# Two reciprocals later on VectorE, one residual sum earlier on GpSimd, and the third norm's squares ahead of four signs on ScalarE

## The reference

```python
qkv = layernorm(x) @ W_qkv.T              # q, k, v per head; k is normalised again per head
# per head, at each of 512 positions t:
F_t = retention * F_{t-1} + coef * v_t k_t^T     # 16 x 16, elementwise factors
y_t = (W_LTM + F_t) q_t
x1  = x + layernorm(y @ W_o.T)
h   = square(relu(layernorm(x1) @ W_fc.T))       # 1024 wide
u   = h @ W_proj.T
# 5 steps of a leaky neuron driven by u; s = spikes / 5
out = x1 + layernorm(s)
```

## Time and profile before

| | us |
|---|---|
| median of 3 runs | 570.86 (570.71 to 573.21) |
| the profiled execution's own time | 573.23 |
| its span, first to last instruction | 571.4 |
| VectorE busy | 514.7 (90% of the span) |
| TensorE busy, matmuls | 478.8 (84%) |
| GpSimd busy | 385.7 (67%) |
| ScalarE busy | 366.4 (64%) |
| mean granted clock of TensorE | 0.914 of full speed |

### The profile page before, as it was taken

How to read it: one execution, slowest core, us unless ns; L and a number is a source line. 1 busy time by engine, 2 the same in 40 slices (tenths; PEclk the granted TensorE clock), 3 DMA queues, 4 the chain that set the end, 5 groups by cost and what they waited for, 6 DMA issues and landing times.

```text
span 571.4 us, 7792 instructions
## 1 busy us (share of the span) xinstructions
PE 478.8 (84%) x2245; PEld 318.6 (56%) x2252; DVE 514.7 (90%) x746; ACT 366.4 (64%) x901; POOL 385.7 (67%) x206
## 2 busy tenths in 40 slices
PE   4683587759999798979898999989997989897992
PEld 2451244426576566736574657656674657465881
DVE  5799999999997999899897999899989998797767
ACT  4561323664677977887768887896879736863331
POOL 1138978687848977696868795888679694783022
PEclk9686557858989999999899999999999989999997
DMA  7475577457484559547774749454934588410002
GB/s 263 130 205 145 147 208 197 147 148 186 135 215 96 149 124 278 146 130 184 216 196 124 177 114 276 143 145 118 285 109 125 153 244 217 111 39 7 30 2 73
DMA packets 54778, 87.64 MB, mean 153 GB/s; under 512 B 5456, under 2 KB 19408, under 8 KB 54736
## 3 DMA queue, kind: packets, MB, share of 16 engines
q1 hardware_dynamic: 54160, 87.12, 56.3%
q10 hardware_dynamic: 576, 0.03, 0.1%
HBM read 78.74 MB, written 8.39 MB: 152 GB/s over the span
## 4 chain that ended last, share of the span: by engine, by line
PE 59%; DVE 15%; issue 9%; ACT 9%; POOL 5%; DMA 1%; SPq 0%; DVEq 0%; ACTq 0%; POOLq 0%
PE p_c L382 15%; PE p_c L412 12%; DVE state L982 8%; PE p_a L312 7%; PE p_y L360 7%; PE p_c L373 6%; POOL prod L1250 4%; PE p_a L333 3%; ACT sign L713 2%; PE p_y L351 2%; PE p_u L552 1%; ACT oo L615 1%; DVE p_u L972 1%; PE p_a L342 1%; DVE yf L1202 1%
## 5 line engine op out<-in xcount | busy, mean ns | idle before, releaser
L1250 POOL TENSOR_TENSOR prod<-state,qf 128x1024 f32<-128x1024 f32 x127 | 300.3, 2380 | 117.6 <-PE p_y L360 69.3
L982 DVE TENSOR_TENSOR_SCAN state<-ret,p_u 128x512 f32<-128x512 f32 x256 | 308.7, 1209 | 0.0
L972 DVE TENSOR_TENSOR p_u<-vrep,p_k 128x512 f32<-128x512 f32 x256 | 171.5, 676 | 0.1
L382 PE MATMUL p_c<-wproj_sb,ht 128*128 128x256 f32 x448 | 100.4, 379 | 0.0
L382 PEld LDWEIGHTS p_c<-wproj_sb,ht 128*128 128x128 f32 x448 | 84.0, 190 | 12.0 <-ACT yf L626 0.8
L312 PE MATMUL p_a<-xt,wqkv_s 128*128 128x512 f32 x276 | 84.8, 448 | 3.0 <-POOL xt L1266 1.6
L412 PE MATMUL p_c<-x1t,wfc_s 128*128 128x512 f32 x324 | 81.6, 398 | 1.8 <-ACT hr L697 1.1
L360 PE MATMUL p_y<-prod,summer 128*32 128x512 f32 x512 | 73.9, 652 | 9.1 <-POOL prod L1250 8.0
L312 PEld LDWEIGHTS p_a<-xt,wqkv_s 128*128 128x128 f32 x276 | 54.9, 208 | 42.1 <-issue 15.5
L412 PEld LDWEIGHTS p_c<-x1t,wfc_s 128*128 128x128 f32 x324 | 59.3, 188 | 22.8 <-issue 7.3
L713 ACT ACTIVATE sign<-yf,drive_sb 128x512 bf16<-128x512 f32 x60 | 38.1, 709 | 0.2
(11 more groups left out here) (190 smaller groups left out, 614.7 us busy)
## 6 DMA issues: line engine op xcount, KB each, us to landing
vrep<-v_rows SPq DMA_DIRECT2D x256, 256.0 KB, 4.7
xa<-in_x SPq DMA_DIRECT2D x9, 512.0 KB, 4.8
v_rows<-vf SPq DMA_DIRECT2D x16, 256.0 KB, 2.5
x<-in_x SPq DMA_DIRECT2D x7, 512.0 KB, 6.8
out<-x SPq DMA_DIRECT2D x7, 512.0 KB, 3.3
ht<-in_w_fc SPq DMA_DIRECT2D x1, 1024.0 KB, 7.6
wproj_sb<-in_w_proj SPq DMA_DIRECT2D x1, 1024.0 KB, 10.3
state<-in_w_qkv SPq DMA_DIRECT2D x1, 512.0 KB, 6.0
```

Source lines behind the costliest of these rows:

```text
L382: last = pe.matmul(p_c[(u + 1) % 2][:, 0:D], ht[:, f, tokens(u)], wproj_sb[:, f, :], start=(f == 0), stop=(f == FT - 1))
L972: v.tensor_tensor(p_u[n % NU][:, :], vrep[:, n % NV, :], p_k[:, :], ALU.mult).then_inc(S["hebb_done"], 1)
L982: v.tensor_tensor_scan(state[:, s % NS, i, :], ret[:, r:r + 1].broadcast_to([P, L]), p_u[n % NU][:, :], 0.0, ALU.mult, ALU.add).then_inc(S ...
L1250: p.tensor_tensor(prod[:, s % NZ, :, :], state[:, s % NS, :, :], qf[:, s // HS, :].unsqueeze(1).broadcast_to([P, 2, L]), ALU.mult).then_in ...
```

## The change

The third norm's reciprocal, `scales(3, b1)`, stays in slot 8 of VectorE's order but moves behind both `hebbian` and the first `scan` of that slot. The first norm's, `scales(1, b)`, moves from slot 3 to slot 4, behind `key_reciprocal(g, 1)`. On GpSimd `add_attention(b1)` moves from slot 6 to slot 5, which is in front of `read(g, 5)` instead of behind it. On ScalarE `squares_x1(b1)` and `deviation(3, b1)` move in front of `copy_yf(b2, 2)` and `copy_key(g)`, and of the five signs of the first pair only one stays before them; the other four come behind `copy_xt(b, 0)`. The second load of x for the last element gets a semaphore of its own, `last_in`, in place of `again_in`. No instruction is added or taken away but for semaphore waits.

```diff
--- before.py
+++ after.py
@@ -162,7 +162,7 @@
         p_c = [ps(f"p_c{i}", [P, L]) for i in range(2)]
 
         S = {name: sem(name) for name in """
-            x_in wv_in wkq_in params_in tables_in weights_in again_in out_done
+            x_in wv_in wkq_in params_in tables_in weights_in again_in last_in out_done
             setup_ready setup_exp wv_high wv_low wk_high wk_low wq_high wq_low wide_high wide_low
             halves_set ones_ready wv_mean wv_centred wkq_mean wkq_centred wide_mean wide_copied wide_centred wo_mean wo_centred tables_done setup_step
             n1_stats n1_sum n1_mean n1_var n1_dev n1_step n1_done  xt_turned xt_done xt_high xt_low
@@ -278,7 +278,7 @@
                     if s == 5 and g >= 1: load_again(g - 1)
                     if s == 6 and g == LAST:
                         sp.wait_ge(S["xt_turned"], KT * B)
-                        sp.dma_start(xa[:, :, :], by_tile(x, LAST)).then_inc(S["again_in"], 16)
+                        sp.dma_start(xa[:, :, :], by_tile(x, LAST)).then_inc(S["last_in"], 16)
                     if s == 13 and g < B - 1: store_v(g + 1, 0)
                     if s == 12 and g < B - 2: load_x(g + 2)
             store_out(B - 3)
@@ -706,13 +706,13 @@
                 act.wait_ge(S["sign_done"], at(2 * (b - 1) + u // 2 + 1))
                 copy(p_c[(u + 1) % 2][:, 0:D], yf[:, u, :], "down_done", TILES * b + u + 1, "yf_done")
 
-            def signs(b, pair):
+            def signs(b, pair, first=0, count=STEPS):
                 act.wait_ge(S["yf_done"], at(TILES * b + 2 * (pair + 1)))
                 act.wait_ge(S["count_done"], at(2 * (b - 1) + pair + 1))
-                for j in range(STEPS):
+                for j in range(first, first + count):
                     last = nc.scalar.activation(sign[:, pair, j, :, :], yf[:, 2 * pair:2 * pair + 2, :], ACT.Sign,
                                                 bias=drive_sb[:, j:j + 1], scale=BELOW_ONE)
-                last.then_inc(S["sign_done"], 1)
+                if first + count == STEPS: last.then_inc(S["sign_done"], 1)
 
             def copy_count(b, pair):
                 act.wait_ge(S["res_done"], at(b))
@@ -811,15 +811,16 @@
                         if before: norm(2, b1, oo, oo, "x1_done", b1)
                         if two_before:
                             copy_yf(b2, 1)
-                            signs(b2, 0)
+                            signs(b2, 0, 0, 1)
                     if s == 6:
+                        if before:
+                            squares_x1(b1)
+                            deviation(3, b1)
                         if two_before: copy_yf(b2, 2)
                     if s == 7:
                         if now: copy_key(g)
-                        if before:
-                            squares_x1(b1)
-                            deviation(3, b1)
                         if after: copy_xt(b, 0)
+                        if two_before: signs(b2, 0, 1, 4)
                     if s == 8:
                         if after: copy_xt(b, 1)
                         if two_before: copy_yf(b2, 3)
@@ -1094,16 +1095,16 @@
                     if now and not first: hebbian(g, s, 0)
                     if s > 0 and now: scan(g, s - 1, 1)
                     if s == 0 and before: scan(b1, SLOTS - 1, 1)
-                    if before and s == 8: scales(3, b1)
                     if now:
                         if first: hebbian(g, s, 0)
                         hebbian(g, s, 1)
                         scan(g, s, 0)
                     if g == 0 and s == 1: tables()
-                    if after and s == 3: scales(1, b)
                     if now and s == 4: key_reciprocal(g, 1)
+                    if after and s == 4: scales(1, b)
                     if before and s == 5: scales(2, b1)
                     if now and s == 6: norm_k(g, 1)
+                    if before and s == 8: scales(3, b1)
                     if two_before and after and s == 13: scales(4, b2)
                     if g == 0 and s == 13: mean_out()
                     if after and s == 13: key_reciprocal(b, 0)
@@ -1141,7 +1142,7 @@
             def tail_attention(pair):
                 dve.wait_ge(S["n2_done"], TILES * LAST)
                 tail_reciprocal(2, 2 * pair, 2, pair + 1)
-                dve.wait_ge(S["again_in"], 16 * B)
+                dve.wait_ge(S["last_in"], 16)
                 for i in range(2):
                     u = 2 * pair + i
                     last = v.scalar_tensor_tensor(xa[:, u, :], part(p_u[pair], i), rdev[1][:, u:u + 1],
@@ -1330,7 +1331,7 @@
                     if g == 0 and s in (5, 6): centre_wide(s - 5)
                     if g == 0 and 10 <= s < 14: low_wide((s - 10) // 2, s % 2)
                     if s == 0 and before: read(b1, SLOTS - 1)
-                    if before and s == 6: add_attention(b1)
+                    if before and s == 5: add_attention(b1)
                     if after and s in (7, 9): low_x(b, (s - 7) // 2)
                     if before and after and s == 10:
                         low_x1(b1, 0)
```

## The result

| | before | after |
|---|---|---|
| median, compared in turn on one chip | 572.86 us (570.41 to 575.81, 20 runs) | 569.48 us (565.06 to 570.75, 20 runs) |
| span of the profiled execution | 571.4 us | 566.5 us |

The ratio is 0.994, with a 95% interval from 0.9922 to 0.9959: 3.4 us faster, between 2.3 and 4.5. The kernel before is 2 us slower in this comparison than in the three runs shown ahead, so the forecast of 569.9 us is near the measured time by luck: its starting point was 2.0 us too low and its difference of 1.0 us was 2.4 us too small, outside the measured 2.3 to 4.5. A second trace of the kernel before has a span of 569.3 us. In iterations 2 to 7 it has as many stretches in which TensorE's granted clock is half of full speed as the trace after (four), and in each of the two traces they lengthen three iterations by 1.6 to 1.7 us.

What follows compares the result with a forecast made beforehand. TensorE and what it waits for, not VectorE, was taken to set the pace. Terms of +0.1 (iteration 1), -1.1 (iteration 7) and 0 (iterations 2 to 6) gave -1.0 us, from 570.86 to 569.9 us; range 567.3 to 572.8.

Steps and rivals of the forecast that it cites:

- What sets the pace: Iterations 2 to 6: TensorE and what it waits for set the pace; VectorE's waits for norms are slack.
- First norm's reciprocal: VectorE, slot 3 to slot 4: its 1.42 us wait goes, but TensorE gains nothing: 0.
- Third norm: Squares earlier, reciprocal later: VectorE leaves slot 8 2.4 us earlier but waits in slots 13 and 15: 0.
- Key copy as the next thing late: VectorE's first hebbian of slot 8 waits for ScalarE's key copy, 1.6 us; 2.4 us in iteration 7.
- Four signs: ScalarE, behind the first turned copy: done 0.3 us before the second turned tile: 0, at most 6.2 us lost.
- Rival B: ScalarE is late at the second turned tile, slowing every middle iteration: up to 6.2 us, 576.1 us; 7%.
- Iteration 1: GpSimd stands 1.7 us longer for the second norm; a later wait takes up all but 0.1: +0.1 us.
- Iteration 7: VectorE goes on 2.4 us earlier; TensorE's 1.06 us wait for its last read goes: 1.1 us gained.
- Sum: Whole kernel: +0.1, -1.1 and 0 in iterations 2 to 6 make -1.0 us.
- Rival C: TensorE's clock falls in other places, 1.7 us each: 566.5 to 573.3 us; 17%.

Runs made afterwards that it cites:

- psum_work: The changed kernel with three more VectorE products in slot 9 of iterations 2 to 6, one operand in PSUM and one in SBUF: 567.35 us.
- squares_only: The changed kernel without its two later reciprocals, both put back where they were: 570.05 us.
- sum_back: The changed kernel with the residual sum behind GpSimd's sixth read again (slot 6): 574.75 us.
- after_more_vector: The changed kernel with three more VectorE products of two SBUF operands in slot 9 of iterations 2 to 6: 587.34 us.
- after_filled: The changed kernel with, in slot 10, TensorE's first up product ahead of the second spike count and GpSimd's low halves of x1 ahead of its read: 568.65 us.

## Why the prediction was right or wrong

- **What sets the pace.** Right: TensorE and what it waits for, not VectorE. 27 us of VectorE's waits went, 2.8 us of time went in the matched pair of traces, and none of that came from VectorE's reciprocals in the middle. psum_work shows it from the other side. The rule of the Trainium skill cited in the prediction ("Perfetto Trace Analysis", "Identifying the Most-Contended Engine") would have sent one to VectorE, 90% busy; here the measurements decide against it.
- **First norm's reciprocal: 0.** Right (squares_only).
- **Third norm: 0 in the middle.** Wrong by 0.18 us in each of five iterations. The reckoning followed ScalarE's turned copy to 363.6 and GpSimd's sum to 359.3, but did not follow GpSimd further: its first low half of x starts 1.0 us earlier in iteration 3, counted from the last `kc` copy (215.88 to 239.32 after, 218.56 to 243.01 before), and so does all that stands behind it, up to the low halves of x1 that TensorE's first up product needs. The list of what TensorE waits for was taken from idle times in brackets, and this wait was not in a bracket.
- **Key copy as the next thing late.** Right in kind and, nearly, in size: 1.94 us, 2.52 in two iterations, where 1.6 was written; 1.96 in iteration 7 for 2.4.
- **Four signs, cover of 0.3 us.** Right: 0.19 us are left. Rival B did not come; in sum_back ScalarE is late for the second turned tile (though there the third norm is late as well), and the time is about 5 us above the changed kernel's.
- **Iteration 1: +0.1.** Its mechanism is there: GpSimd waits 1.4 us for the second norm, and TensorE waits 0.86 us for the low half, 0.1 more than before. But in the matched pair the iteration is 0.3 us shorter, and what of that is the clock is open.
- **Iteration 7: -1.1.** Mis-sized: -1.39. VectorE's last read came in time and the 1.06 us wait went, but two sums in one go also overlap where they had stood apart (1.92 us for both against 2 x 1.06). The 0.14 us left lie ahead of the sums, 0.11 of them at the turning of x1 behind the third norm; why was not tested. The reciprocal itself is not it: before, it was ready at 488.9, and the norm began at 490.50.
- **Sum.** -0.9 (five times 0.18) - 1.4 in place of 0 - 1.1; with 0.5 us of iterations 0 and 1, whose cause is open, that makes the pair's 2.8 us. The measured 3.4 us has an interval of 2.3 to 4.5 that holds it; no cause for the rest was looked for beyond the clock.
- **Rival C** was real, but in the pair of traces of one kernel it acted in iterations 0 and 1. Its price of 1.7 us for each stretch was too simple: of the two stretches in iteration 4 one cost nothing.

## What to carry to other kernels

Follow a transfer or a result that comes earlier through every engine's order until something takes it up. An instruction that starts within 0.1 us after another engine ended what it needs may have waited for it, even where the profile prints no idle time. A wait can also be cover for something else: the wait for the signs took up a half-clock stretch. Ask of every wait to be removed what the engine meets next: here 27 us of waits were worth 2.8 us. An engine's slack is best measured by giving it harmless work, of a form that takes no resource from the others.

## What the runs showed of the hardware

- A VectorE product of 128x512 with two SBUF operands took 1.76 us at the median (0.74 to 2.84) beside GpSimd's products (after_more_vector), with one operand in PSUM 0.68 us (psum_work).
- TensorE's granted clock differed in iterations 0 and 1 between two executions of one kernel (0.64 and 0.79 against 0.66 and 0.85): 2 us of time. In after_filled it fell to half once or twice in every middle iteration, though TensorE stood for less of it (4.6 us of 61.5, against 5.6 of 60.7 in the changed kernel at full clock).
- A half-clock stretch cost 1.7 us near the start of an iteration (62.53 against 60.87 us, before) and nothing just ahead of a wait of TensorE (60.67 us, squares_only).
